# A DLRM tower on one core: the gram of a tile in two halves, and the last but one chunk finished in the last phase

## What is computed

```python
e = jnp.stack([tbl_0[ids[:, 0]], ..., tbl_25[ids[:, 25]]], axis=1)      # (2048, 26, 128)
sd = jnp.einsum('bfd,bd->bf', e, dense)
ss = jnp.einsum('bfd,bgd->bfg', e, e)
z = jnp.concatenate([dense, sd, ss[:, iu, ju]], axis=1)                  # iu, ju: upper triangle
h = jnp.concatenate([z, dense], axis=1)
h = jnp.maximum(h @ W_top1 + b_top1, 0.0)                                # 607 -> 512
h = jnp.maximum(h @ W_top2 + b_top2, 0.0)                                # 512 -> 256
y = h @ W_top3                                                           # 256 -> 1
```

## Time and profile before

| | |
|---|---|
| runs, median (lowest to highest) | 394.25 us (394.03 to 397.19) |
| the profiled execution | 390.34 us, span 388.5 us |
| mean granted clock of TensorE | 0.952 |
| PE busy | 325.2 us, 84% of the span |
| DVE busy | 223.5 us, 58% |
| ACT busy | 188.1 us, 48% |
| POOL busy | 263.9 us, 68% |
| DMA | 44.48 MB, 114 GB/s |

### The profile page before, as it was taken

How to read it: one execution, slowest core, us unless ns; L and a number is a source line. 1 busy time by engine, 2 the same in 40 slices (tenths; PEclk the granted TensorE clock), 3 DMA queues, 4 the chain that set the end, 5 groups by cost and what they waited for, 6 DMA issues and landing times.

```text
span 388.5 us, 14097 instructions
## 1 busy us (share of the span) xinstructions
PE 325.2 (84%) x6128; PEld 300.9 (77%) x6128; DVE 223.5 (58%) x655; ACT 188.1 (48%) x282; POOL 263.9 (68%) x283
## 2 busy tenths in 40 slices
PE   0875888877989898989899798979899798987756
PEld 0765786767989797978799698968799697977745
DVE  1999869645854694557467385547466574503011
ACT  2346563714655464536445464535455463546122
POOL 5777677777777777777777777777777777760020
PEclk9999899955999999999999899998999998999699
DMA  7998633554345443653264434543265435420130
GB/s 177 241 243 247 199 86 76 128 140 105 92 108 128 122 109 72 146 138 82 79 146 136 96 88 104 136 115 84 80 142 141 102 79 113 122 58 3 33 84 0
DMA packets 44639, 44.48 MB, mean 114 GB/s; under 512 B 28738, under 2 KB 34326, under 8 KB 44577
## 3 DMA queue, kind: packets, MB, share of 16 engines
q1 hardware_dynamic: 34350, 25.23, 26.8%
q0 software_dynamic: 8832, 18.00, 18.3%
q10 hardware_dynamic: 1394, 0.35, 0.4%
HBM read 38.01 MB, written 5.55 MB: 112 GB/s over the span
## 4 chain that ended last, share of the span: by engine, by line
PE 70%; DVE 10%; issue 9%; DMA 7%; ACT 3%; SPq 1%; ACTq 0%; DVEq 0%
PE et_ps L528 30%; PE g_ps L547 14%; PE m_ps L504 12%; PE et_ps L520 7%; DVE one_hot L444 7%; PE m_ps L571 5%; DMA et<-tbl_in 4%; PE m_ps L580 1%; DMA gram_rows<-gram 1%; DMA idb<-ids_one_hot 1%; DVE table_lo L433 1%; ACT et L367 1%; DMA zt_raw<-gram_rows 1%; DVE w_lo L429 1%; DVE w_hi L427 1%
## 5 line engine op out<-in xcount | busy, mean ns | idle before, releaser
L325 POOL DMA_INDIRECT rows<-tbl_in,idx x272 | 260.8, 959 | 86.4 <-issue 77.2
L444 DVE TENSOR_SCALAR one_hot<-idb,first_row 125x256 fp32r<-125x256 int32 x576 | 181.5, 385 | 73.5 <-PE et_ps L528 39.5
L528 PE MATMUL et_ps<-one_hot,table_hi 125*128 125x256 f32 x576 | 156.5, 306 | 21.5 <-DVE one_hot L444 17.6
L528 PE MATMUL et_ps<-one_hot,table_lo 125*128 125x256 f32 x576 | 148.3, 291 | 0.0
L528 PEld LDWEIGHTS et_ps<-one_hot,table_hi 125*128 125x128 f32 x576 | 115.1, 200 | 27.2 <-issue 15.9
L528 PEld LDWEIGHTS et_ps<-one_hot,table_lo 125*128 125x128 f32 x576 | 115.4, 200 | 0.1
L367 ACT COPY et<-et_ps 128x384 f32<-128x384 f32 (+1 forms) x80 | 86.5, 1085 | 41.7 <-PE et_ps L520 39.9
L547 PE MATMUL g_ps<-et 128*27 128x26 f32 x4096 | 58.6, 196 | 29.7 <-issue 22.1
L547 PEld LDWEIGHTS g_ps<-et 128*27 128x27 f32 x4096 | 47.9, 107 | 41.3 <-issue 34.5
L359 ACT COPY et<-et_ps 128x256 f32<-128x256 f32 (+1 forms) x80 | 44.3, 675 | 39.4 <-PE et_ps L528 39.4
L380 ACT COPY gram<-g_ps 128x416 f32<-128x416 f32 x32 | 28.5, 889 | 66.6 <-PE g_ps L547 66.6
(11 more groups left out here) (44 smaller groups left out, 215.8 us busy)
## 6 DMA issues: line engine op xcount, KB each, us to landing
idb<-ids_one_hot SPq DMA_DIRECT2D x32, 256.0 KB
gram_rows<-gram SPq DMA_DIRECT2D x30, 169.0 KB
rows<-tbl_in,idx POOLq DMA_INDIRECT x272
et<-tbl_in SPq DMA_DIRECT2D x6, 448.0 KB
xt<-dense_t SPq DMA_DIRECT2D x8, 128.0 KB
idb<-ids_one_hot SPq DMA_DIRECT2D x8, 128.0 KB
raw<-tbl_in SPq DMA_DIRECT2D x2, 448.0 KB
zt_raw<-gram_rows SPq DMA_DIRECT2D x15, 48.0 KB
```

The lines of the kernel that those rows point to most:

```text
L325: nc.gpsimd.indirect_dma_start(out=rows[:, i % ROW_RING, n, :], out_offset=None, in_=tables[GATHERED[k]], in_offset=bass.IndirectOffsetOnA ...
L444: nc.vector.tensor_scalar(one_hot[0:KP, at % OH_RING, :], idb[0:KP, pair % ID_RING, n % 2, :], first_row[0:KP, 0:1], float(k), ALU.subtrac ...
L528: last = nc.tensor.matmul(ps[:, n % 2 * CH:(n % 2 + 1) * CH], part[0:KP, n, k, :], one_hot[0:KP, at % OH_RING, :], start=k == 0 and part i ...
```

## The change

Only the three lists of words change. In PHASE and LAST, X0 moves from behind G7 to between G5 and G6. K2 moves from behind O7 to behind T4. In PHASE, O0 of the next chunk and M0 now stand between G1 and G2, where M0 stood ahead of G0 and O0 behind T5; T5 and T6 now follow G3. In LAST, T5 and M0 stand between G1 and G2. The layers m0 and y0 of chunk 6, which TAIL held, stand before and behind T9 in LAST. In TAIL x0 (chunk 7) moves from behind D8 to between G5 and G6. The number of steps and their work stay the same.

```diff
 PHASE = (
-    "O4 Z0 Z1 G4 G5 G6 G7 X0 Z2 W0 T0 O5 K0 T1 D0 D1 O6 K1 D2 D3 T2 D4 D5 O7 K2 T3 D6 D7 D8 O8 T4 M0 G0 "
-    "G1 G2 G3 T5 O0 T6 Y0 O1 T7 O2 T8 O3 T9").split()
+    "O4 Z0 Z1 G4 G5 X0 G6 G7 Z2 W0 T0 O5 K0 T1 D0 D1 O6 K1 D2 D3 T2 D4 D5 O7 T3 D6 D7 D8 O8 T4 K2 G0 G1 "
+    "O0 M0 G2 G3 T5 T6 Y0 O1 T7 O2 T8 O3 T9").split()
...
 TAIL = (
-    "G4 G5 G6 G7 W0 M0 Y0 D0 D1 D2 D3 D4 D5 D6 D7 D8 x0 z0 k0 z1 k1 z2 k2 m0 y0").split()
+    "G4 G5 x0 G6 G7 W0 D0 D1 D2 D3 D4 D5 D6 D7 D8 z0 k0 z1 k1 z2 k2 m0 y0").split()
```

More of the change, by code:

```diff
@@ L31 @@
 PHASE = (
-    "O4 Z0 Z1 G4 G5 G6 G7 X0 Z2 W0 T0 O5 K0 T1 D0 D1 O6 K1 D2 D3 T2 D4 D5 O7 K2 T3 D6 D7 D8 O8 T4 M0 G0 "
-    "G1 G2 G3 T5 O0 T6 Y0 O1 T7 O2 T8 O3 T9").split()
+    "O4 Z0 Z1 G4 G5 X0 G6 G7 Z2 W0 T0 O5 K0 T1 D0 D1 O6 K1 D2 D3 T2 D4 D5 O7 T3 D6 D7 D8 O8 T4 K2 G0 G1 "
+    "O0 M0 G2 G3 T5 T6 Y0 O1 T7 O2 T8 O3 T9").split()
 LAST = (
-    "O4 Z0 Z1 G4 G5 G6 G7 X0 Z2 W0 T0 O5 K0 T1 D0 D1 O6 K1 D2 D3 T2 D4 D5 O7 K2 T3 D6 D7 D8 O8 T4 M0 G0 "
-    "G1 G2 G3 T5 Y0 T6 z0 z1 x0 k0 z2 T7 k1 k2 T8 T9").split()
+    "O4 Z0 Z1 G4 G5 X0 G6 G7 Z2 W0 T0 O5 K0 T1 D0 D1 O6 K1 D2 D3 T2 D4 D5 O7 T3 D6 D7 D8 O8 T4 K2 G0 G1 "
+    "T5 M0 G2 G3 Y0 T6 z0 z1 x0 k0 z2 T7 k1 k2 T8 m0 T9 y0").split()
 TAIL = (
-    "G4 G5 G6 G7 W0 M0 Y0 D0 D1 D2 D3 D4 D5 D6 D7 D8 x0 z0 k0 z1 k1 z2 k2 m0 y0").split()
+    "G4 G5 x0 G6 G7 W0 D0 D1 D2 D3 D4 D5 D6 D7 D8 z0 k0 z1 k1 z2 k2 m0 y0").split()
 AHEAD = 4
```

## The result

The changed kernel takes 405.09 us (median of four runs, of which one took 973.86 us; the other three 403.20, 404.72 and 405.46), the kernel before 395.72 beside it. The runs of one kernel differ by several microseconds, so ratios with an interval compare the means of the runs within 1.5% of the fastest, and those marked "of medians" all runs: here the ratio is 1.0235, 95% interval 1.0148 to 1.0323. In a later session the same two gave medians of 403.96 and 396.47, ratio 1.0216 (1.0136 to 1.0295). So the change costs 8.4 to 9.3 us; the prediction's sum was +6.9 and its time 401. The profiled execution took 404.72 us, span 402.9, clock 0.945. That is 14.4 us over the span of 388.5 before, more than the runs differ: the profiled execution of before, 390.34 us, lies 3.7 us under the fastest run beside it.

A forecast was written before the change was run, and what follows sets the result against it. TensorE's order of work, with gaps in the gram, was taken to bound the kernel. Terms -3.7 + 6.5 + 1.0 - 0.1 + 0.5 + 2.7 gave +6.9 us on the 388.5 span, hence 401; 8-in-10 range 391 to 408.

The forecast's parts named there:

- the term for the start-up: Phases 0 and 1 up to the first steady period: -2.9, -1.3 and +0.5, together -3.7 us.
- the gap: Waits inside the gram, 12 totalling 15.4 us between 100 and 330 us, read as instruction code that has not arrived.
- the gaps stay: Rival: a refill's wait belongs to each 256 instructions whatever lies between, 11 us more, 412; chance 0.05.
- Steps 1 to 3: Steady phase from G7 to M0: O0 waits for late ids, h_lo queues behind its one-hots; 2.5 us lost.
- the walk: The prediction's unit-by-unit timing of one steady phase after the change, from the end of G7; 44.0 us a phase.
- Step 4: Steady phase, M0 to Y0: Y0 waits 0.8 us for M0's relu, queued on ScalarE behind the copies of xt.
- Step 5: Steady phase, O1 to O2: O2 waits for the copies that empty O0/O1's PSUM bank; 1.25 us lost.
- Step 6: Rest of the steady phase to G7: remaining code gaps in the gram halves kept at 0.4 us a phase.
- Low clock in the phases: Lower TensorE clock behind waits in the five steady phases: +1 us, bounds -3 and +7.
- the rival of a low clock in each phase: O0 and M0 at half rate in all five phases, 1.5 us more each, 408; chance 0.12.
- Last phase and tail: From T4(7) to the end: -0.1 last phase, +0.5 for G4 to G7, +2.7 for K blocks at the lower clock.
- The ids come in time: Rival: O0's one-hots start by 16 us after G7, saving time until gathers limit it to -4, about 390; chance 0.15.

The follow-up runs named there:

- e7_halves: Kernel before with only the gram halved: X0 between G5 and G6, T5 and O0 (T5 and Y0 in the last phase) between G1 and G2; 385.09 us, ratio 0.9846.
- e9_gapfill: Kernel before, old order, plus 12 idle products in each of eleven places inside the gram; 389.20 us, ratio 0.9824 to before.
- e11_k2: Changed kernel with K2 put back behind O7; 403.51 us, ratio 1.0221 to before.
- e1_ids: Changed kernel with the ids' load for the next O0 issued ahead of the six zt_raw reads; 394.55 us, ratio 0.991 to before, of medians.
- e2_bank: Changed kernel with T5 ahead of O0 in the steady phases, so O2 takes T5's bank; 397.55 us, ratio 1.0055 to before.
- e4_new_end: Kernel before with only the last phase and tail (LAST and TAIL) of the changed kernel; 398.92 us, ratio 1.009 to before.
- e0_after: The changed kernel itself, run again in a later session as a measure; 403.96 us, ratio 1.0216 to before.
- e8_fill: Changed kernel plus 68 idle products in the tail while TensorE is empty; 402.88 us, ratio 1.019 to before, of medians, two runs.
- e3_old_end: Changed kernel with LAST and TAIL as before the change, only the steady phases new; 402.20 us, ratio 1.0195 to before.
- e10_halves_fill: Kernel of e7_halves plus 24 idle products in the tail, between x0 and z0; 383.86 us, ratio 0.9703 to before.

## Why the prediction was right, and where it was not

The forecast was slower, 401 in a range of 391 to 408, and it came out slower at 405.1 (404.0 later). The direction and the mechanisms of the steady phases were right; the term for the start-up had the wrong sign. Point by point:

- **What bounds the kernel; the gap.** Right. Splitting a gram takes most of its gaps away (15.4 to 1.8 us, and 3.5 in e7_halves), and e9_gapfill shows them to be waits that other work can cover. The sentence of the Trainium skill ("Runtime: NRT & Kernel Launch", Instruction fetch mechanics) that crossing such a block is mostly hidden holds, by that reading, for O and K here, not for the gram. That the gaps are code is still a reading from the sizes; no run shows what arrives in them. The rival "the gaps stay" is out.
- **Steps 1 to 3, the ids.** Right in mechanism, less in size per wait: VectorE started 17.8 us after G7 where 17.5 stood, but O0 waited about 1.3 us in four of five phases and 0.2 was lost at M0, where the step had 2.5 in all. TensorE reaches O0 later than the walk said, for which e11_k2 is a measure: 1.2 us later and hardly a wait is left. e1_ids takes the loss away and gives back 7.7 us in five periods, 1.5 each.
- **Step 4, Y0.** 0.4 us by the row against 0.8. **Step 5, O2's bank:** 1.1 us in each phase by the row, 1.4 by the starts of the units, against 1.25. But its repair gave back only 1.4 us in five periods (e2_bank), since Y0 and the gram wait longer instead: in the steady phases most of this wait is covered by others.
- **Step 6, the remaining gaps.** Too small: I kept 0.4 a phase. The row has 1.8 us in the gram, but the chain shows many short stops in it (G2 and G3 took 3.1 us in phase 3, where I had 1.85), and 3.4 us moved into O and T. That makes up for the waits, which were shorter than the walk's. The five periods together: 44.0 and 1 for the clock, +7.5, predicted; +8.7 measured between the two profiles, +2.3 against e4_new_end.
- **Low clock in the phases.** Taken as +1; the mean clock of after is 0.956 in four runs (e0_after), that of before 0.950 beside it. In the two profiles it is 0.98 over the five periods of either. It did not add to the loss, and the rival of a low clock in each phase is out. The gaps of before lower it, as e9_gapfill shows; that they go was a gain that the sum had only as the lower bound of this term.
- **Start-up, the step that failed.** The prediction had -3.7: -2.9 in phase 0, with no bank wait in it at all, -1.3 in phase 1, where "the bank wait of O2 costs less than that beside units that run at the lower clock anyway", and +0.5. Measured is +1.0 against before, and +4.1 against e4_new_end. The bank wait that was left out or taken as hidden costs 4.7 between after and e2_bank: 1.74 us idle in phase 0 (ScalarE copies xt, the gram, T5 and T6 before the pair, 4.6 us in a row with the pair), the lower clock behind it, and another such wait (1.41 us) in phase 1; how much of the 4.7 is clock the profiles don't divide. Without it, e2_bank's last product of G7(1) starts 3.7 us before that of before, the number of the prediction, but by luck: phase 0 gave -1.0 of the -2.9, phase 1 made up for it, and against e4_new_end the difference is only -0.6.
- **Last phase and tail.** From G7(6) to G4(7) +0.9 where -0.1 stood; G4 to G7 +1.5 where +0.5 stood, as gaps of 1.40 and 0.64 us stayed in it, the longer one ahead of X0. The lower clock under the last blocks and what follows them: +2.3 against the +2.7 of the prediction, and e8_fill shows that it comes from the empty TensorE. It was no certain loss, though: with the old end the last blocks already began at the lower clock in e3_old_end and e7_halves (11.5 us instead of 10.04). In the runs the price of the new end is 1% (e4_new_end). The Trainium skill ("TensorE: Matmul & The Clock Gate", What's actually happening), by which activity releases the throttle, agrees with this trace: 0.50 under the K blocks behind 11.4 us without a product, 1.00 with the fill.
- **Sum.** Between the profiles it is +14.4 and not +6.9: 4.7 of the difference is the start-up, 1.2 the periods, 1.0 and 1.0 the last phase, and -0.4 the tail. In the runs it is +8.4 to +9.3. That the sum lies near the runs is in part luck: the profile that it was worked out on took 3.9 us less than the median of its runs, and set against e4_new_end the start-up is off by 7.8 us and the periods by 5.2 the other way.
- **The rival that ends faster.** "The ids come in time" was priced at 390, with a floor by the gathers. e1_ids, which makes exactly that true, came out at 3.6 us less than before by medians, where the rival had 4; since the rival's sum holds the start-up's -3.7, which e1_ids does not have (110.2 at G7(1)), that closeness is luck too. The floor was right: the last gather lands 1.5 us after its end (I took 2), and once the waits are gone, in e10_halves_fill, GpSimd has 44% of the chain.

## What to carry to other kernels

Very dense runs of small products can stand still in gaps that no semaphore explains (here probably for their own code); put other work between them, or even idle products, but look at which loads and which bank copies the work that moves forward depends on, for the in-order queues behind them stay where they were. Before you count a bank wait as hidden, add up what its copying engine has queued ahead of that copy; here it was seven copies, 4.6 us. When the last work before an unavoidable wait is moved away, the layers behind that wait can start at the lower clock. And before you divide a loss among the parts of a kernel, look how far two profiles of the same order of work lie apart in each part; here it was 3 and 6 us.

## What the runs showed of the hardware

- The gram's gaps, 15.4 us between 100 and 330 us, fall to 3.8 when 11 blocks of 12 idle products are put in, with no longer time: the engine was waiting for something that arrives at its own pace.
- More work can be faster: with 132 added products the time fell by 1.8%, with a mean granted clock of 0.974 instead of 0.950. The fit over the runs of before is 2.8 us for each 0.01 of clock.
- Two profiles of the same order of work differ in clock and time by stretch: 0.91 and 0.97 over the first 110 us (3.1 us apart), 0.98 and 0.95 over the five periods (6.4 us apart the other way).
- A TensorE without a product for 11.4 us comes back at the lower clock: 22 products in 4.8 us, against 36 in 5.3. Behind 2.7 us without a product the same blocks ran at 1.00 in before; behind 3.6 and 3.2 us at 0.72 in e3_old_end and in e7_halves; behind 3.5 us, with the idle products ahead of it, at 1.00 in e8_fill.
- A gather of 128 rows holds GpSimd for 0.94 us with 0.30 us behind it, and its data lands 2.45 us after its start.
